# Expert 0 of a mixture-of-experts forward pass: half of its first layer computed in Strassen form, like the other seven experts

## The reference, cut to what matters

```python
h = relu(einsum('bi,eio->beo', x, eW1) + eb1)
h = relu(einsum('beh,eho->beo', h, eW2) + eb2)
expert_out = einsum('beh,eho->beo', h, eW3) + eb3
gates = softmax(einsum('bi,tie->bte', x, gW) + gb, axis=-1)
tin = einsum('bte,bed->btd', gates, expert_out)
th = relu(einsum('btd,tdh->bth', tin, tW1) + tb1)
th = relu(einsum('bth,tho->bto', th, tW2) + tb2)
out = sigmoid(einsum('bth,tho->bto', th, tW3) + tb3)[..., 0]
```

## Time and profile before

| what | value |
|---|---|
| median of three runs | 574.85 us (574.71 to 574.85) |
| the profiled execution's own time | 574.77 us |
| its span, first to last instruction | 573.0 us |
| mean granted TensorE clock | 1.000 of full speed (2.4 GHz) |
| PE busy | 568.1 us, 99% of the span |
| DVE busy | 443.4 us, 77% |
| ACT busy | 306.4 us, 53% |
| POOL busy | 96.6 us, 17% |
| chain that ended last | PE 98%, ACT 1%, DVE 1% |
| HBM read | 85.10 MB |

### The profile page before, as it was taken

How to read it: one execution, slowest core, us unless ns; L and a number is a source line. 1 busy time by engine, 2 the same in 40 slices (tenths; PEclk the granted TensorE clock), 3 DMA queues, 4 the chain that set the end, 5 groups by cost and what they waited for, 6 DMA issues and landing times.

```text
span 573.0 us, 8424 instructions
## 1 busy us (share of the span) xinstructions
PE 568.1 (99%) x2867; PEld 477.6 (83%) x2867; DVE 443.4 (77%) x556; ACT 306.4 (53%) x414; POOL 96.6 (17%) x102
## 2 busy tenths in 40 slices
PE   9999999999999999999999999999999999999998
PEld 5788888888888888888888888888888888888776
DVE  7955479975997869976799759977699768998493
ACT  3545366634673375733665356733757246654553
POOL 0002211042102411033200521024110332004000
DMA  8534774466726675466654567265744676426100
GB/s 309 180 110 115 183 201 100 148 164 195 175 81 178 181 170 130 146 165 176 190 118 151 157 185 176 75 198 171 173 115 146 165 198 177 119 73 209 49 1 0
DMA packets 39422, 85.30 MB, mean 149 GB/s; under 512 B 3425, under 2 KB 8673, under 8 KB 39410
## 3 DMA queue, kind: packets, MB, share of 16 engines
q1 hardware_dynamic: 29986, 65.98, 34.2%
q0 software_dynamic: 9280, 18.91, 19.0%
q10 hardware_dynamic: 144, 0.26, 0.1%
HBM read 85.10 MB, written 0.04 MB: 149 GB/s over the span
## 4 chain that ended last, share of the span: by engine, by line
PE 98%; ACT 1%; DVE 1%; issue 0%; ACTq 0%
PE psum L464 32%; PE psum L467 16%; PE psum L320 16%; PE psum L321 16%; PE psum L322 16%; PE psum L586 1%; PE psum L448 1%; PE psum L564 0%; ACT w_hi L876 0%; ACT scratch L911 0%; PE psum L650 0%; DVE w_lo L921 0%; DVE scratch L1225 0%; ACT h_hi L786 0%; DVE x_both L1237 0%
## 5 line engine op out<-in xcount | busy, mean ns | idle before, releaser
L921 DVE TENSOR_TENSOR w_lo<-w_raw,w_hi 128x1024 fp32r<-128x1024 f32 (+2 forms) x106 | 138.0, 1305 | 21.9 <-ACT w_hi L728 12.7
L320 PE MATMUL psum<-h_hi,w_hi 128*128 128x512 f32 (+1 forms) x340 | 131.8, 388 | 0.8 <-DVE h_lo L932 0.8
L321 PE MATMUL psum<-h_lo,w_hi 128*128 128x512 f32 (+1 forms) x340 | 131.6, 387 | 0.0
L322 PE MATMUL psum<-h_hi,w_lo 128*128 128x512 f32 (+1 forms) x340 | 131.4, 387 | 0.0
L464 PE MATMUL psum<-t_both,w_hi 128*128 128x512 f32 x448 | 122.1, 394 | 0.0
L464 PE MATMUL psum<-x_both,w_hi 128*128 128x512 f32 x336 | 91.6, 394 | 0.0
L932 DVE SCALAR_TENSOR_TENSOR h_lo<-scratch,h_hi 128x512 fp32r<-128x512 f32 (+1 forms) x68 | 67.0, 988 | 27.2 <-ACT scratch L787 19.5
L464 PEld LDWEIGHTS psum<-t_both,w_hi 128*128 128x128 f32 x448 | 77.0, 189 | 10.8
L1287 POOL DMA_DIRECT2D w_raw<-eW_pairs x28 | 24.2, 865 | 350.6 <-DMA w_raw<-eW_pairs 349.9
L467 PEld LDWEIGHTS psum<-t_both,w_lo 128*128 128x128 f32 x448 | 68.8, 189 | 9.5
L320 PEld LDWEIGHTS psum<-h_hi,w_hi 128*128 128x128 f32 x340 | 63.9, 188 | 14.0 <-DVE h_lo L932 1.2
(11 more groups left out here) (99 smaller groups left out, 625.0 us busy)
## 6 DMA issues: line engine op xcount, KB each, us to landing
w_raw<-eW_pairs SPq DMA_DIRECT2D x28, 768.0 KB, 4.2
w_raw<-eW SPq DMA_DIRECT2D x40, 512.0 KB, 4.0
scratch<-eW_pairs SPq DMA_DIRECT2D x28, 256.0 KB, 4.8
w_raw<-eW_pairs SPq DMA_DIRECT2D x28, 256.0 KB, 5.1
w_raw<-eW_pairs POOLq DMA_DIRECT2D x28, 256.0 KB, 4.7
scratch<-eW_pairs POOLq DMA_DIRECT2D x28, 256.0 KB, 6.5
scratch<-gates_dram POOLq DMA_DIRECT2D x8, 512.0 KB, 5.4
w_raw<-eW_first SPq DMA_DIRECT2D x6, 512.0 KB, 6.6
```

What stands on the lines that cost most here:

```text
L320: pe.matmul(bank, weights_hi, moving_hi, start=first, stop=False)
L321: pe.matmul(bank, weights_hi, moving_lo, start=False, stop=False)
L322: return pe.matmul(bank, weights_lo, moving_hi, start=False, stop=last)
L921: dve.tensor_tensor(wide(w_lo, slots), raw, wide(w_hi, slots).bitcast(F32), ALU.subtract).then_inc(slot_ready, 1)
```

## The change

Expert 0 keeps one plain group: the four tiles 0, 4, 1, 5 of the outputs (pairs 0 and 1), from weight pieces 0 to 3. Pairs 2 and 3 are computed in Strassen form by `pair(0, 2)` and `pair(0, 3)`, with their weights laid out and loaded as those of later experts. G1 (A11, A12 and S1) is one cast and one subtraction of 1536 columns. `turn_logits` moves to between the two pairs and waits for all four staged tiles, `turn_gates` to behind pair 3. P4 of pair 3 stands behind the first two steps of layer 2. The sums t use two buffers of four blocks each instead of four, so that `sum_x(2)` and `sum_x(3)` wait for `split_t(0)` and `split_t(1)`. SP loads the blocks of pair 2 after two splits and those of pair 3 after four, then W2 of expert 0 after G3 and G4 of each pair, then expert 1's first blocks after the second split of W2. POOL issues the four accumulating DMAs of pairs 2 and 3 of expert 0 ahead of expert 1's. PSUM banks and places in `scratch` move accordingly. A function `nth(e, i)` counts pairs from expert 0's pair 2 on and replaces `PAIRS * (e - 1) + i` in all counts of semaphores. The loop over experts 1 to 7 and the towers have the same instructions as before.

The core of the diff:

```diff
--- before.py
+++ after.py
-SPLITS0 = KX + 4
+GROUP = [0, 4, 1, 5]
+PIECES = KX // 2
+PIECE_SLOT = [4, 2, 6, 0]
+FIRST_PAIR = 2
+FIRST_ORDER = [(p, i) for p, i in IN_ORDER if i >= FIRST_PAIR]
+FIRST_SPLITS = [("G1", 2), ("G2", 2), ("G3", 2), ("G1", 3), ("G4", 2), ("G2", 3), ("G3", 3),
+                ("W2", 0), ("G4", 3), ("W2", 1), ("W2", 2), ("W2", 3)]
+SPLITS0 = PIECES + len(FIRST_SPLITS)
...
-BANK_HIDDEN1 = [0, 1, 2, 3, 5, 6, 7, 4]
+BANK_GROUP = [4, 1, 6, 7]
 BANK_HIDDEN2 = [5, 6, 7, 4]
 BANK_OUT3 = [0, 1]
-BANK_LOGITS, BANK_TURNED, BANK_GATES = 4, 0, 1
+BANK_LOGITS, BANK_TURNED, BANK_GATES = 5, 7, 0
...
-        t_raw = scratch[:, KX * BATCH:2 * KX * BATCH].rearrange("p (k b) -> p k b", k=KX)
+        t_raw = scratch[:, KX * BATCH:(KX + KK) * BATCH].rearrange("p (s k b) -> p s k b", s=2, k=KK)
...
-        X_SUMS = [((0, 0), False, (0, 1), (0, 0)),
-                  ((1, 1), False, (0, 1), (0, 1)),
-                  ((0, 0), True, (1, 1), (1, 1)),
-                  ((1, 1), True, (1, 0), (1, 0))]
+        X_SUMS = [((0, 0), (0, 1), (0, 0), 0),
+                  (None, (1, 1), (1, 1), 1),
+                  (None, (1, 0), (1, 0), 0),
+                  ((1, 1), (0, 1), (0, 1), 1)]
...
-            for j in range(2, KX):
-                if j < KX // 2:
-                    for k in (2 * j, 2 * j + 1):
-                        sp.dma_start(x_raw[:, k, :], x_dram[k]).then_inc(x_landed[k], DMA)
-                if j >= UNITS:
-                    sp.wait_ge(slot_ready, j - UNITS + 1)
-                sp.dma_start(halves(j % UNITS), first_dram(j)).then_inc(landed[j % UNITS], DMA)
-                if j == KX // 2 - 2:
+            for j in range(2, PIECES):
+                for k in (2 * j, 2 * j + 1):
+                    sp.dma_start(x_raw[:, k, :], x_dram[k]).then_inc(x_landed[k], DMA)
+                sp.dma_start(halves(j), first_dram(j)).then_inc(landed[j], DMA)
+                if j == PIECES - 2:
                     sp.dma_start(prm[:], small).then_inc(small_landed, DMA)
-            for i in range(4):
-                sp.wait_ge(slot_ready, 5 + i)
-                sp.dma_start(halves(i), w2_piece_dram(0, i)).then_inc(landed[i], DMA)
-            sp.wait_ge(t_ready, NX)
-            sp.wait_ge(slot_ready, splits(1) - 2)
+            for i in range(FIRST_PAIR, PAIRS):
+                sp.wait_ge(slot_ready, 2 * (i - FIRST_PAIR + 1))
+                load_blocks(0, i)
+                load_a22(0, i)
+            for n, what in enumerate([("G3", 2), ("G4", 2), ("G3", 3), ("G4", 3)]):
+                sp.wait_ge(slot_ready, split(0, *what))
+                load_w2(0, n)
+            sp.wait_ge(slot_ready, split(0, "W2", 1))
...
+                elif first and i == FIRST_PAIR:
+                    pe.wait_ge(logitsT_ready, 1)
+                elif first:
+                    pe.wait_ge(h1_staged, 2)
                 product(e, "P2", i)
+                if first:
+                    if i == FIRST_PAIR:
+                        pe.wait_ge(t_ready, 1)
                 if i == 0:
...
+                if first and i == FIRST_PAIR:
+                    pe.wait_ge(t_ready, 2)
...
+                    if first and (n, m) == (2, 0):
+                        last_product(e, PAIRS - 1)
...
-                pe.wait_ge(h1_staged, 1)
+                pe.wait_ge(h1_staged, MG)
...
-            between = {(0, 6): gate_logits, (1, 4): turn_logits, (1, 6): turn_gates}
-            first_group(0, range(1, KX), between)
-            first_group(1, range(KX), between)
+            first_group()
+            pair(0, 2)
+            turn_logits()
+            pair(0, 3)
+            turn_gates()
             layer2(0)
-            pe.wait_ge(t_ready, NX)
-            pe.wait_ge(h1_staged, MG)
             with nc.Fori(1, E, engines=(PE,), hint_back_edge=True) as e:
...
-            for n in range(NX):
-                t_cast(n)
-            first_hi(5)
+            t_cast(0)
+            t_cast(1)
+            g1_hi(0, 2)
+            t_cast(2)
+            t_cast(3)
             act.wait_ge(small_landed, DMA)
-            for m in range(MG):
-                take_first(m)
-            first_hi(6)
-            first_hi(7)
+            g2_hi(0, 2)
+            g3_hi(0, 2)
+            take_first(0)
+            n1_take(0, 2)
+            take_first(1)
+            p5_take(0, 2)
+            g1_hi(0, 3)
+            n2_take(0, 2)
+            take_first(2)
+            take_first(3)
+            g4_hi(0, 2)
+            g2_hi(0, 3)
+            g3_hi(0, 3)
+            n1_take(0, 3)
+            w2_hi(0, 0)
+            p5_take(0, 3)
+            g4_hi(0, 3)
+            n2_take(0, 3)
             act.wait_ge(soft, 4)
             act.activation(gate[:], logit[:], ACT.Exp).then_inc(exp_done, 1)
-            first_w2_hi(0)
-            first_w2_hi(1)
-            for m in range(MG, 2 * MG):
-                take_first(m)
-            first_w2_hi(2)
-            first_w2_hi(3)
+            c21_take(0, 2)
+            pair_h1(0, 2)
+            w2_hi(0, 1)
+            w2_hi(0, 2)
+            c21_take(0, 3)
+            w2_hi(0, 3)
+            pair_h1(0, 3)
...
-                    dve.scalar_tensor_tensor(block_of(t_raw, *place), block_of(t_raw, *a), -1.0, block_of(x_raw, *b),
+                    dve.wait_ge(t_ready, n - 1)
+                if a is None:
+                    dve.wait_ge(x_sum, n)
+                    dve.scalar_tensor_tensor(t_raw[:, at, :, :], t_raw[:, 1 - at, :, :], -1.0, block_of(x_raw, *b),
...
-            first_lo(4)
-            for n in range(NX):
-                sum_x(n)
+            sum_x(0)
+            sum_x(1)
+            split_t(0)
+            sum_x(2)
+            split_t(1)
+            sum2(0, 2)
+            g1_lo(0, 2)
+            sum_x(3)
             dve.wait_ge(logits_done, 1)
             dve.tensor_copy(turned, banks[BANK_LOGITS]).then_inc(logitsT_ready, 1)
-            for n in range(NX):
-                split_t(n)
-            first_lo(5)
-            for m in range(MG):
-                first_h1_lo(m)
-            first_lo(6)
-            first_lo(7)
+            sum4(0, 2)
+            g2_lo(0, 2)
+            split_t(2)
+            split_t(3)
+            g3_lo(0, 2)
+            c11_sum(0, 2)
+            sum2(0, 3)
+            g1_lo(0, 3)
+            first_h1_lo(0)
+            first_h1_lo(1)
+            c12_sum(0, 2)
+            sum4(0, 3)
+            first_h1_lo(2)
+            c22_sum(0, 2)
+            g4_lo(0, 2)
+            g2_lo(0, 3)
+            first_h1_lo(3)
+            g3_lo(0, 3)
+            upper_fold(0, 2)
+            lower_fold(0, 2)
+            c11_sum(0, 3)
...
+            w2_lo(0, 0)
+            g4_lo(0, 3)
...
-            first_w2_lo(0)
+            c12_sum(0, 3)
+            c22_sum(0, 3)
+            c21_fold(0, 2)
+            pair_h1_lo(0, 2)
+            w2_lo(0, 1)
+            w2_lo(0, 2)
             dve.wait_ge(gates_turned, 1)
             dve.tensor_copy(turned[0:T * E, :], banks[BANK_GATES][0:T * E, :]).then_inc(gated_ready, 1)
-            first_w2_lo(1)
-            for m in range(MG, 2 * MG):
-                first_h1_lo(m)
-            first_w2_lo(2)
-            first_w2_lo(3)
+            upper_fold(0, 3)
+            lower_fold(0, 3)
+            c21_fold(0, 3)
+            w2_lo(0, 3)
+            pair_h1_lo(0, 3)
...
+            sum_blocks(0, 2)
+            sum_blocks(0, 3)
             sum_blocks(1, 0)
             pool.wait_ge(t_ready, NX)
-            pool.wait_ge(h1_ready, K2)
+            pool.wait_ge(h1_ready, MG)
...
-    w1 = np.asarray(L0_rec_eW1)[1:].reshape(E - 1, 2, KK, P, 2, PAIRS, P)
+    w1 = np.asarray(L0_rec_eW1).reshape(E, 2, KK, P, 2, PAIRS, P)
     pairs = np.stack([w1[:, kh, :, :, mh] for mh, kh in BLOCKS], axis=0).transpose(1, 4, 3, 0, 2, 5)
-    pairs = pairs.reshape(E - 1, PAIRS, P, len(BLOCKS) * KK * P)
+    pairs = pairs.reshape(E, PAIRS, P, len(BLOCKS) * KK * P)
+    first = np.asarray(L0_rec_eW1)[0].reshape(D, K2, P)[:, GROUP].reshape(D, MG * P)
```

More of the change, by code:

```diff
@@ L116, with nth @@
 NSMALL = _at
+def nth(e, i):
+    return PAIRS * (e - 1) + i + (PAIRS - FIRST_PAIR)
 def used(e, product):
+    if isinstance(e, int) and e == 0:
+        at = FIRST_ORDER.index(product)
+        return PIECES_USED + at + 1 + (2 if at == len(FIRST_ORDER) - 1 else 0)
     return USED0 + (e - 1) * USED + AT[product] + 1
@@ L133, in split @@
 def split(e, *what):
+    if isinstance(e, int) and e == 0:
+        return PIECES + FIRST_SPLITS.index(what) + 1
     return splits(e) + SPLIT_ORDER.index(what) + 1
@@ L471, in pair @@
             def pair(e, i):
-                if i == PAIRS - 1:
-                    pe.wait_ge(combined, PAIRS * (e - 1) + 1)
+                first = isinstance(e, int)
+                if i == PAIRS - 1 and not first:
+                    pe.wait_ge(combined, nth(e, 0) + 1)
                 elif i == 1:
@@ L683, in take_first @@
                     act.wait_ge(x_sum, NX)
[L684 removed]
```

(33 more changed lines are left out.)

227 lines of the change are left out of this document (108 added, 119 removed).

## The result

The median over 15 runs is 576.93 us (574.63 to 579.15), against 574.92 us (574.71 to 575.46) for the kernel before in 15 runs on the same chip: ratio 1.0034 [1.0024, 1.0044]. The change makes the kernel slower by 0.34%. The forecast was 574.0 us, inside 573.1 to 576.6; the result has the other sign and lies just above the range. The spread also grew from 0.8 us to 4.5 us.

The account below looks back on a forecast made before the run. PE, busy 99% of the span, was taken as the bound: 2.26 us less work, minus waits of 0.8 and 0.6, gains 0.84 us, so 574.77 becomes 573.93, and with the median 0.08 above, 574.0 us (range 573.1 to 576.6).

Parts of the forecast that it names:

- PE's work: Expert 0's pairs 2 and 3: 14 products, 19.6 us, replace 21.86; gain 2.26 us if PE never waits.
- First wait: At turn_logits between pairs 2 and 3: PE waits for all four staged tiles, 37.74 to 38.5, 0.8 us.
- Second wait: At turn_gates behind pair 3: PE waits for DVE's packed splits, sums and softmax, 48.75 to 49.35, 0.6 us.
- the sum: From pair 2's start at 29.34, products, transposes, two waits and layer 2 added up to expert 1 beginning at 73.05.
- POOL issues the accumulation of S1, which lands 4.1 to 6.4 us later: Expert 0's pair 2: S1 lands at 21.4 to 23.7, taken as 22.2, before DVE reaches sum2 at 23.9.
- an issue among other loads: The old trace's S1 issue at 63.54, landed after 4.5 us; used to support S1 of pair 2 landing at 22.2.
- rival 1: At g1_hi(0, 2) and sum2(0, 2): S1 of pair 2 lands late, at 28.2, giving 578.2 us; chance of loss 0.13.
- the free limit of 24.0: S1 of expert 0's pair 2: from a landing at 24.0 on, each us of delay costs PE 1 us.
- these cost nothing while that cover holds: Expert 1's loads and POOL's queue: blocks issued at 54.4, S1 by 65.2 for 73.05; memsets and gates' stores behind, no cost.

Follow-up runs that it names:

- both late runs: The changed kernel, 576.93 us, and the changed kernel with POOL issuing expert 1 pair 1's accumulations before its wait for the stored gates, 574.93 us.
- with the first cause gone: Against the changed kernel, DVE adds S1 of expert 0's pair 2 in place of POOL's accumulating DMA: 576.03 us, ratio 1.0019.
- with the second gone: Against the changed kernel, POOL issues S1 and S3 of expert 1's pair 1 before waiting for the stored gates: 574.93 us, ratio 0.9995.
- with both: Against the changed kernel, SP loads pair 3 after G1 of pair 2 is split, and POOL issues expert 1 pair 1's accumulations earlier: 574.6 us, ratio 0.9992.

## Why the prediction was wrong

**PE's work: right.** Fourteen products at 1.40 us: in the changed kernel P1 of pair 3 to `turn_gates` is 51.92 - 41.63 = 10.29 us for seven products and one wait, and layer 2 with P4 75.55 - 52.27 = 23.28 where 23.26 were forecast.

**First wait: right.** 0.75 us for 0.8, released by the staged copy on ACT as said. It was 0.7 in every version that left the transpose there, with pair 2 delayed or not.

**Second wait: a little too long.** The row says 0.25 us for 0.6. By the starts the difference is smaller: seven products and the wait took 10.29 us, against 9.8 + 0.6 = 10.4, so 0.5 went there, half of it not put down to a wait. Likewise the first wait, by the starts, is 41.25 - 38.84 - 1.40 = 1.0 us for 0.8. The two errors have opposite signs and nearly cancel, which is luck. With S1 of pair 2 added by DVE, the way from the first product of pair 2 to expert 1 took 73.10 - 29.52 = 43.58 us; the sum had 73.05 - 29.34 = 43.71. As a sum over the engines the forecast held to 0.13 us.

**The step that failed first: "POOL issues the accumulation of S1, which lands 4.1 to 6.4 us later", "I take 22.2".** It was issued at 17.08, where 17.1 was forecast for its blocks, and landed at 26.67. (From 17.1 the range would be 21.2 to 23.5; the 21.4 to 23.7 of the sum are 0.2 too late, which decides nothing.) I took the range of 28 landings as a bound, and the 4.5 us of the earlier trace rows as that of "an issue among other loads"; but that issue, at 63.54, has SP's nearest load 4.4 us ahead of it, and the new one has it 0.19 behind. None of the 28 has a load of SP's issued between 1.5 us ahead of it and 1.0 behind, and the six longest, 6.1 to 6.4, are those right behind a load of the gates in POOL's own queue. The range said nothing about the case that the change made. The place and the price were those of rival 1, and it named two causes: of these, DVE without a gap is refuted (4.5 us under the same unbroken DVE work, 4.2 under the additions in the kernel before), and pair 3's 1.25 MB in the same engines is what the runs show. The price per us also held. From the free limit of 24.0 on each us was to cost PE one: P7 of pair 2 starts 12.17 us behind the landing in both late runs (38.84 for 26.67, 37.23 for 25.06), so a free landing is one 5.17 us ahead of the end of group 0, which on the old clock is 24.2. The landing at 26.67 gave 38.84 - 30.00 + 0.15 - 7.00 = 1.99 us lost on pair 2 (0.15 is the late start of P1), the one at 25.06 gave 1.12. The rest of expert 1's lateness, 0.5 us, is the start: group 0 ended at 29.85 instead of 29.34 in this run.

**The step that failed second, and cost more: "these cost nothing while that cover holds".** I followed S1 of expert 1's *pair 0* through POOL's queue, and it did land 8.6 us ahead of its use (66.94 for 75.55). The S1 behind it, of *pair 1*, stands on the same queue behind the stores of the gates, the wait for them and their load. In the old trace S1 of pair 1 was issued 10.2 us after that of pair 0, in the new one 10.8; the wait for the stores is 5.56 us of it instead of 2.48, with SP's loads (62.11) now issued beside the accumulations ahead of it. But S1 of pair 0 is itself 8.0 us later (61.34 for 53.30), since SP's loads of expert 1 are, while PE's clock moved by 1.7. So S1 of pair 1 is issued 6.9 us nearer to its use, SP's next loads follow it 1.26 us later, and it takes 9.1 us to land. On ACT the cast that waits for it stands ahead of a `p5_take` of the pair before. ACT was ready for that cast at 78.25 (81.20 less 2.95 idle), 6.1 us after the issue, so by this sum the late issue alone, with a landing of 4 to 5 us, would have cost nothing; the late issue and the long landing had to meet. The prediction's own rule was to name what is queued behind a step that moves; it named the memsets and the stores and stopped one instruction short.

**How much each is worth.** By the ratios: 1.0034 as it is; 1.0019 [1.0004, 1.0034] with the first cause gone; 0.9995 [0.9986, 1.0004] with the second gone; 0.9992 [0.9983, 1.0001] with both. The second is worth 2.2 us in the median. The first comes to about 0.9 alone, but the two intervals overlap, so its worth is shown in the profiles and not in the medians; what it adds once the second is gone cannot be told from nothing either. With the second gone the time is back at the old one although S1 of pair 2 still lands late: a forecast whose first step was wrong would have been inside its range there, by luck. The spread is 4.4 us with only the first gone, 2.5 with only the second gone and 1.1 with both; that it comes from which of two queues issues first within some tenths of a us fits this, and is not shown.

**The rule weighed.** The Trainium skill ("SBUF — State Buffer", section "SBUF: two separate sides") has a DVE instruction in a two-port mode keep GpSimd from writing its DMAs' descriptors. I applied it to all of DVE's list. The runs show that additions and subtractions with two inputs in SBUF, which are what fills the stretch, delay nothing: 4.2 us under 16 of them in a row. The section itself, under "Who interferes with whom", lets copies, casts and `tensor_scalar` enter two-port modes and gives `tensor_tensor` none, and agrees so far; a long run of copies was not tried. On the queues, the Trainium skill ("DMA: Bandwidth & Descriptors", section "Queues, rings and completion order") says that each DMA engine goes round its queues packet by packet. Where both queues have packets the trace is not far from that (48.0 and 44.9% of the engines between 22 and 23 us, 67.7 and 33.1 between 78 and 79). But for 4 us after the issue POOL's queue shows no packet at all, while SP's has up to 96%. Whether its packets were held back there or not yet ready, no run shows.

## What to carry to other kernels

In these runs an accumulating DMA of 256 KB that lands 4 to 5 us after its issue when it is alone took 7.7 to 9.6 when another queue issued 1.25 MB (768, 256 and 256 KB) beginning within some 0.4 us of it, and 8.9 to 9.4 with 768 KB and more beginning 1.2 us behind it when its own queue held a load ahead of it. A range of landings read off a trace holds only for the neighbours that they had there, so look for the load nearest to each landing before using it as a bound. When a change moves a stage on one queue, follow that queue past the first item you are interested in, up to the first one that the bounding engine's helpers wait for; and when two such landings decide, move one of the two issues apart from the other. Moving SP's load brought the first landing from 9.6 to 4.5 us; putting one accumulation ahead of a wait that it does not need brought the second from 9.1 to 4.4, and was worth as much (2.2 us) as all the arithmetic that the change saves.
